# Fourth layer of a graph network: the last 16 node tiles as two groups of 8, and 416 instead of 352 byte pairs on ScalarE in steps 4 to 39

## The reference

```
h = relu(layernorm(x))
layer 0: x += relu((adj @ h) @ W.T + b)
layer 1: x += points and sigmoid attention on a hyperboloid, weighted by adj, normed
layer 2: agg_i = sum_j adj_ij / deg_i * logmap(h_i, h_j)       # Poincare ball, all pairs
         x += expmap(0, agg @ W2 + b2)                          # tanh of the length
layer 3: support = h @ W3;  mask = (adj != 0);  rank = cumsum(mask, axis=1)
         deg = rank[:, -1:];  k = min(deg, 100);  pos = rank - (deg - k)
         w = mask * where(pos > 0, 0.5 ** (k - pos), 0);  x += w @ support + b3
```

## Time and profile before

| | us |
|---|---|
| median of 3 runs | 1047.3 (1044.82 to 1051.48) |
| profiled execution, its own time | 1044.31 |
| its span, first to last instruction | 1042.6 |
| PE busy | 980.6 (94%) |
| DVE busy | 850.0 (82%) |
| ACT busy | 750.8 (72%) |
| POOL busy | 298.0 (29%) |
| mean granted TensorE clock | 0.981 |

### The profile page before, as it was taken

One profiled execution on the slowest core, in us unless ns is written; L12 is line 12 of the kernel. 1 busy time (PEld: TensorE's weight loads), 2 busy tenths in 40 slices (PEclk: granted clock), 3 DMA queues, 4 the chain that ended last, 5 costly groups with the idle time before them and its releaser, 6 DMA issues.

```text
span 1042.6 us, 16458 instructions
## 1 busy us (share of the span) xinstructions
PE 980.6 (94%) x6171; PEld 475.1 (46%) x6171; DVE 850.0 (82%) x1080; ACT 750.8 (72%) x805; POOL 298.0 (29%) x140
## 2 busy tenths in 40 slices
PE   6999979999899999999989999999999999998888
PEld 2444444446644444435434444444455454333455
DVE  6999969998678676697769987878878978888883
ACT  4655545554477667686788989988888888997683
POOL 1069980000001000004015464434343444342001
PEclk9999989999989999999998999999999999999999
DMA  9989987994048899788753444555655553446662
GB/s 330 420 332 422 423 366 241 345 403 162 1 160 282 292 304 301 262 268 303 261 188 127 160 127 158 170 194 164 198 163 162 165 171 116 155 142 201 214 217 78
DMA packets 96350, 238.43 MB, mean 229 GB/s; under 512 B 16401, under 2 KB 45073, under 8 KB 79889
## 3 DMA queue, kind: packets, MB, share of 16 engines
q1 hardware_dynamic: 87056, 220.62, 61.5%
q10 hardware_dynamic: 9216, 16.78, 4.2%
HBM read 219.55 MB, written 17.83 MB: 228 GB/s over the span
## 4 chain that ended last, share of the span: by engine, by line
PE 62%; DVE 20%; ACT 9%; issue 7%; POOL 1%; DMA 1%; DVEq 0%; SPq 0%; ACTq 0%; POOLq 0%
PE PS L577 39%; PE PS L756 9%; DVE TB L1559 6%; PE PS L896 4%; PE PS L865 4%; DVE work L2078 2%; ACT work L1268 2%; ACT work L1276 2%; DVE work L2066 2%; DVE ring L2084 1%; ACT work L1279 1%; DVE work L2072 1%; PE PS L589 1%; DVE work L1729 1%; ACT work L1262 1%
## 5 line engine op out<-in xcount | busy, mean ns | idle before, releaser
L555 POOL TENSOR_TENSOR ring<-work,ring 128x1024 f32<-128x1024 f32 x57 | 135.3, 2374 | 232.8 <-DVE work L2078 232.7
L1729 DVE TENSOR_TENSOR work<-work,ring 128x1024 f32<-128x1024 f32 x128 | 152.9, 1234 | 58.0 <-ACT work L1193 57.9
L1193 ACT ACTIVATE work<-PS,att_sc 128x1024 f32<-128x1024 f32 x128 | 148.0, 1201 | 68.5 <-PE PS L756 59.5
L1118 ACT ACTIVATE work<-PS 128x1024 uint8<-128x1024 f32 x128 | 124.2, 1024 | 100.0 <-PE PS L577 99.9
L577 PE MATMUL PS<-ring,work 128*65 128x256 f32 (+1 forms) x600 | 190.4, 465 | 3.8 <-DVE work L2105 3.8
L577 PE MATMUL PS<-work 128*64 128x512 f32 (+2 forms) x800 | 151.5, 519 | 1.4 <-ACT work L1262 1.2
L2072 DVE SCALAR_TENSOR_TENSOR work<-PS,work 128x1024 f32<-128x1024 f32 x72 | 88.0, 1222 | 55.0 <-PE PS L577 46.5
L756 PE MATMUL PS<-work 128*64 128x512 f16 x1024 | 124.0, 384 | 3.0 <-ACT work L1193 1.6
L577 PEld LDWEIGHTS PS<-ring,work 128*65 128x65 f32 x600 | 80.6, 138 | 90.7 <-issue 65.5
L1268 ACT ACTIVATE work<-work 128x1024 f32<-128x1024 f32 x72 | 76.0, 1055 | 34.8 <-DVE work L2066 34.7
L756 PEld LDWEIGHTS PS<-work 128*64 128x64 f16 x1024 | 59.0, 111 | 79.4 <-issue 34.7
(11 more groups left out here) (280 smaller groups left out, 1402.1 us busy)
## 6 DMA issues: line engine op xcount, KB each, us to landing
ring<-in_adj_t SPq DMA_DIRECT2D x96, 1024.0 KB, 5.4
ring<-in_adj_t SPq DMA_DIRECT2D x104, 512.0 KB, 4.1
work<-in_adj_t SPq DMA_DIRECT2D x32, 1024.0 KB, 8.6
codes<-work ACTq DMA_DIRECT2D x64, 256.0 KB, 7.2
ring<-codes SPq DMA_DIRECT2D x64, 256.0 KB, 4.6
H<-in_adj_t SPq DMA_DIRECT2D x24, 512.0 KB, 4.2
X<-in_x SPq DMA_DIRECT2D x2, 256.0 KB, 5.2
X<-in_x SPq DMA_DIRECT2D x1, 512.0 KB, 10.4
```

Source lines behind the costliest of these rows:

```text
L555: nc.gpsimd.tensor_tensor(near(n), sums(n), near(n), ALU.mult).then_inc(sem("near_ready"), 1)
L1118: nc.scalar.activation(made[:, k, u:HALF:2], PS[:, (4 + 2 * u) * BANK:(6 + 2 * u) * BANK], ACT.Relu).then_inc(sem("codes_made"), 1)
L1193: nc.scalar.activation(att[:, u, :], PS[:, (4 + 2 * u) * BANK:(6 + 2 * u) * BANK], ACT.Sigmoid, bias=att_sc[:, 2:3], scale=att_sc[:, 1:2]) ...
L1729: V.tensor_tensor(prob[:, m % 4, :], att[:, u, :], ring[:, s % RING, u * UNIT:(u + 1) * UNIT], ALU.mult)\
```

## The change

Group (16, 32) becomes (16, 24) and (24, 32). Tiles 16 to 23 are complete after unit 65, so that PE gathers them in unit 69 (nodes2(2)), ACT copies them in unit 70, and DVE does tangent_dot and tangent_scale in unit 71, the other tangent operations behind conversion 1. Every call of steps 3 to 5 above now comes twice, once for 8 tiles each, at new places in the three queues. Group 2 has steps 32 to 47 and group 3 48 to 63, so half 0 is complete only after step 55: the copy on ACT moves behind the conversions, and PE's to_nodes from step 52 to step 60. Apart from that, in steps 4 to 39 ACT converts 416 byte pairs (832 elements) and DVE 608. The last product of groups 1 and 3 uses bank 3, that of group 2 bank 2. Nothing else is changed, and the result is computed as before.

```diff
...
-GROUPS = ((0, 8), (8, 16), (16, 32))
+GROUPS = ((0, 8), (8, 16), (16, 24), (24, 32))
...
 PIECES = ((24, 32), (16, 24), (0, 16))
-COMPLETE = (36, 52, 72)
-COPIES = (2, 4, 7)
+COMPLETE = (36, 52, 66, 72)
+COPIES = (2, 4, 6, 8)
+LAST_BANK = (1, 3, 2, 3)
 VISITS = {38: ("agg2_copied", 2), 41: ("turned_out", 1), 42: ("z_out", 1), 51: ("turned_out", 2), 52: ("z_out", 2),
-  54: ("agg2_copied", 4), 57: ("turned_out", 3), 58: ("z_out", 3)}
+  54: ("agg2_copied", 4), 57: ("turned_out", 3), 58: ("z_out", 3), 69: ("agg2_copied", 6)}
+TANGENTS = (1, 3, 4, 6)
+LASTS = (2, 5, 7, 8)
 CAUGHT = 16
...
 POW_A = 352
+POW_A_EARLY = 416
+
+
+def pairs_a(q):
+    return POW_A_EARLY if 4 <= q < 40 else POW_A
 BF_SHIFT = 7
...
 a, b = GROUPS[q]
-bank = (1, 3 if last else 1, 2)[q]
+bank = LAST_BANK[q] if last else 1
 return PS[:, bank * BANK:bank * BANK + (b - a) * D].rearrange("p (t c) -> p t c", c=D)
...
     a, b = GROUPS[q]
-    bank = (1, 3 if b_row is None else 1, 2)[q]
+    bank = LAST_BANK[q] if b_row is None else 1
     for u in range((b - a) // 2):
...
 def weighted(q):
-    pe.wait_ge(sem("turned_out"), 2 * q + 1)
+    pe.wait_ge(sem("turned_out"), TANGENTS[q])
     through(q, wbd["w2"][:, :], 4)
...
     pe.wait_ge(sem("feats_ready_l3"), q + 1)
-    turn(q, cen, 3 if q == 1 else 0)
+    turn(q, cen, LAST_BANK[q] if q else 0)
 def weighted_last(q):
-    pe.wait_ge(sem("turned_out"), 2 * q + 2)
+    pe.wait_ge(sem("turned_out"), LASTS[q])
     pe.wait_ge(sem("w3_done"), 2)
...
         weighted(1)
+    if n == 69:
+        nodes2(2)
...
+    if q == 1:
+        pe.wait_ge(sem("agg2_copied"), COPIES[2])
+        to_tangent(2)
     if q == 2:
...
     if q == 3:
+        weighted(2)
+    if q == 4:
         pe.wait_ge(sem("far_out"), mirrors(NU - 1))
-        nodes2(2)
-    if q == 4:
         to_last(1)
+    if q == 5:
+        pe.wait_ge(sem("z_out"), TANGENTS[2])
+        nodes2(3)
     if q == 6:
         weighted_last(1)
-    if q == 8:
-        pe.wait_ge(sem("agg2_copied"), COPIES[2])
-        to_tangent(2)
     if q == 10:
-        pe.wait_ge(sem("z_out"), 4)
-        weighted(2)
-    if q == 25:
+        pe.wait_ge(sem("agg2_copied"), COPIES[3])
+        to_tangent(3)
+    if q == 12:
+        weighted(3)
+    if q == 19:
         to_last(2)
-    if q == 27:
+    if q == 21:
         weighted_last(2)
-    if q == 52:
+    if q == 32:
+        pe.wait_ge(sem("z_out"), LASTS[1])
+        to_last(3)
+    if q == 34:
+        weighted_last(3)
+    if q == 60:
         pe.wait_ge(sem("sums_out3_a"), 1)
...
+def last_a(q, k):
+    one("part_a", S3(*GROUPS[q], 0), linear_out(q, True), ACT.Copy, ("through", k))
+
...
         root_part("v_root", "v_norm2", 1, 1)
+    if n == 70:
+        nodes2_out(2)
...
         root_part("ln_sd", "ln_var", 3 * G + 1 + 1, 1)
+    if q == 4:
+        turned_out(2, 4)
+    if q == 5:
+        z_out(2, 4)
+        v_square(2, 4)
     if q == 7:
-        nodes2_out(2)
+        turned_out(1, 5, 3)
     if q == 8:
-        turned_out(1, 4, 3)
-    if q == 10:
-        z_out(1, 4, last=True)
-        part_a(1, 4)
-    if q == 13:
-        turned_out(2, 5)
-    if q == 15:
-        z_out(2, 5)
-        v_square(2, 5)
+        nodes2_out(3)
+        root_part("v_root", "v_norm2", 2, 2)
+    if q == 9:
+        z_out(1, 5, last=True)
+        part_a(1, 5)
+    if q == 12:
+        turned_out(3, 6)
+    if q == 14:
+        z_out(3, 6)
+        v_square(3, 6)
+        ln_square(2)
+    if q == 16:
+        root_part("ln_sd", "ln_var", 3 * G + 1 + 2, 2)
     if q == 19:
-        root_part("v_root", "v_norm2", 2, 2)
-    if q == 26:
-        ln_square(2)
+        root_part("v_root", "v_norm2", 3, 3)
+    if q == 22:
+        turned_out(2, 7, 2)
+    if q == 24:
+        last_a(2, 7)
+    if q == 25:
+        ln_square(3)
     if q == 28:
-        root_part("ln_sd", "ln_var", 3 * G + 1 + 2, 2)
-    if q == 29:
-        turned_out(2, 6)
-    if q == 30:
-        one("part_a", S3(*GROUPS[2], 0), linear_out(2), ACT.Copy, ("through", 6))
-    if q == 56:
-        one("sums_out3_a", TA[:, 0:UNIT], PS[:, 4 * BANK:6 * BANK], ACT.Copy, ("agg3_done", 48),
-            scale=W_SCALE / (F16_TOP / LN_TOP))
+        root_part("ln_sd", "ln_var", 3 * G + 1 + 3, 3)
+    if q == 36:
+        turned_out(3, 8, 3)
+    if q == 38:
+        last_a(3, 8)
...
         act.wait_ge(sem("agg2_near"), NU - 2)
-    both = pw(q).bitcast(I16).rearrange("p (u n) -> p u n", u=2)[:, :, 0:POW_A]
-    nc.scalar.activation(both, code(q).rearrange("p (n u) -> p u n", u=2)[:, :, 0:POW_A], ACT.Copy, scale=BF_STEP)\
+    both = pw(q).bitcast(I16).rearrange("p (u n) -> p u n", u=2)[:, :, 0:pairs_a(q)]
+    nc.scalar.activation(both, code(q).rearrange("p (n u) -> p u n", u=2)[:, :, 0:pairs_a(q)], ACT.Copy, scale=BF_STEP)\
       .then_inc(sem("pw_ready_a"), 1)
...
     power(q)
+one("sums_out3_a", TA[:, 0:UNIT], PS[:, 4 * BANK:6 * BANK], ACT.Copy, ("agg3_done", 56),
+    scale=W_SCALE / (F16_TOP / LN_TOP))
 one("sums_out3_a", TA[:, UNIT:UNIT + BANK], banks(6, 7), ACT.Copy, ("agg3_done", 2 * T),
...
         centre3(1)
+    if n == 71:
+        tangent_dot(2)
+        tangent_scale(2)
...
         dve.wait_ge(sem("agg2_near"), NU - 2)
-    two = code(q).bitcast(U16)[:, POW_A:UNIT]
-    V.tensor_scalar(pw(q)[:, POW_A:UNIT].bitcast(U16), two, 0xFF, BF_SHIFT, ALU.bitwise_and, ALU.logical_shift_left)\
+    a = pairs_a(q)
+    two = code(q).bitcast(U16)[:, a:UNIT]
+    V.tensor_scalar(pw(q)[:, a:UNIT].bitcast(U16), two, 0xFF, BF_SHIFT, ALU.bitwise_and, ALU.logical_shift_left)\
      .then_inc(sem("pw_ready_v"), 1)
-    V.tensor_scalar(pw(q)[:, UNIT + POW_A:2 * UNIT].bitcast(U16), two, 1, 0xFF << BF_SHIFT, ALU.logical_shift_right,
+    V.tensor_scalar(pw(q)[:, UNIT + a:2 * UNIT].bitcast(U16), two, 1, 0xFF << BF_SHIFT, ALU.logical_shift_right,
                     ALU.bitwise_and).then_inc(sem("pw_ready_v"), 1)
...
 power(1)
+tangent_part(2)
+tangent_own(2)
+tangent_sum(2)
+power(2)
 spread3(1)
-power(2)
+power(3)
 feats3(1)
-power(3)
 near2_out(n)
+def last_rest(q):
+    dve.wait_ge(sem("part_a"), q + 1)
+    V.tensor_tensor(S3(*GROUPS[q], 1), linear_out(q, True), S3(*GROUPS[q], 0), ALU.subtract)\
+     .then_inc(sem("parts3_ready"), 1)
+
 def last_passage3(q):
-    if q == 10:
-        tangent_dot(2)
-        tangent_scale(2)
-        tangent_part(2)
-        tangent_own(2)
-        tangent_sum(2)
-        rest3(1)
-    if q == 20:
+    if q == 8:
         length(2)
         tanh_num(2, 0, 5)
-    if q == 21:
+    if q == 10:
         length_root(2)
         tanh_den(2)
+    if q == 11:
         tanh_end(2)
-    if q == 22:
+        rest3(1)
+    if q == 12:
+        tangent_dot(3)
+        tangent_scale(3)
+    if q == 13:
+        tangent_part(3)
+        tangent_own(3)
+        tangent_sum(3)
+    if q == 14:
         step_v(2)
         step_x(2)
-    if q == 23:
+    if q == 15:
         mean3(2)
         centre3(2)
+    if q == 17:
+        spread3(2)
+    if q == 18:
+        length(3)
+        tanh_num(3, 0, 5)
+    if q == 19:
+        feats3(2)
+    if q == 21:
+        length_root(3)
+        tanh_den(3)
+    if q == 22:
+        tanh_end(3)
+    if q == 23:
+        step_v(3)
+        step_x(3)
+    if q == 24:
+        mean3(3)
+        centre3(3)
     if q == 25:
-        spread3(2)
-    if q == 26:
-        feats3(2)
-    if q == 29:
-        dve.wait_ge(sem("part_a"), 3)
-        V.tensor_tensor(S3(*GROUPS[2], 1), linear_out(2), S3(*GROUPS[2], 0), ALU.subtract)\
-         .then_inc(sem("parts3_ready"), 1)
+        last_rest(2)
+    if q == 28:
+        spread3(3)
+    if q == 30:
+        feats3(3)
+    if q == 40:
+        last_rest(3)
```

## The result

The changed kernel takes 1051.88 us (median of 20 runs, 1045.33 to 1057.65), the kernel before, on the same chip, 1047.26 (20 runs, 1044.77 to 1052.21). The ratio is 1.0045 with a 95% interval of 1.0028 to 1.0062, or 4.7 us slower (2.9 to 6.5). That is within 1%, and 1.4 us above the forecast.

The account below looks back on a forecast made before the run. PE was taken to be held in the fourth layer by waits, mostly on DVE, between steps 10 and 29. The sum, +1.4 at step 29 and +1.8 behind it, +3.2 us on the median 1047.3, gave 1050.5 us, range 1044 to 1056.

Parts of the forecast that it names:

- the rival with two low stretches: Fourth layer: the longer PE waits bring one to two more stretches at the low clock, 1052 to 1055 us; chance 0.25.
- Gather in unit 69, +1.8: End of third layer: group 2's gather on PE, ahead of unit 71's scores, lengthens the unit loop by 1.8 us.
- Dot and scale ahead of the entry, +1.8: DVE, unit 71: group 2's two operations ahead of the read-out PE waits for delay its entry by 1.8 us.
- Wait of 2.7 at step 1: Before step 1: PE waits 2.7 us for DVE's tangents of group 2, there at 957.3, turning at 960.0.
- Wait of 4.5 at step 10: Before step 10: PE, ready at 974.8, waits 4.5 us for DVE's tangents of group 3, ready at 979.2.
- the other side: Faster outcome if DVE reaches group 3's tangents early enough at step 10: 1041.3 to 1046 us; chance 0.2.
- Steps 10 to 29, -3.4: Between these steps the change gains: PE's waits fall from 8.1 to 4.7 us, leaving +1.4 at step 29.
- Behind 29, +1.8: After step 29: group 3's turn 0.5, its last product 1.0 and waits 0.3 come now, +1.8 us.
- 416 pairs, nothing: Steps 4 to 39: ACT's extra 3.8 us and DVE's saved 1.3 cancel; same end within 0.1 us as with 352.
- the prediction's three signs of being wrong: PE reaches the second turn after DVE; the unit loop doesn't lengthen; the low clock stands where no wait follows.
- the wait at step 10 is not there: Rival: DVE's 19.2 us to group 3's tangents are 14.8 or fewer, 1046.0 or down to 1041.3 us; chance 0.2.
- The hidden gather: Rival: the gather in unit 69 costs nothing, so 1.8 us fall away, +1.4, 1048.7 us; chance 0.15.

Follow-up runs that it names:

- the reordered change: Changed kernel, groups of 8, gather in unit 69 and 416 pairs kept, with only its fourth-layer calls placed anew; ratio to the kernel before 0.9994.
- the reordered kernel: Kernel before, group of 16 kept, with its fourth-layer calls at other steps on PE, ACT and DVE; ratios to the kernel before 0.9954 and, repeated, 0.9966.

## Why the prediction came out as it did

The side and the size of the time were right: 1050.5 forecast, 1051.9 measured, with most of the chance on a time within 1%. By the stretch, which can be set against the working, the sum has less than half of what was measured: +3.2 forecast, +6.9 in the profiled pair. Of the 3.7 us that it lacks, 1.3 arise ahead of step 10, 2.3 between steps 10 and 29. That the time comes within 1.4 us of the forecast is therefore partly luck; it lies closer still to the 1052 to 1055 of the rival with two low stretches. (The count by waits in the working gives 16.7 - 13.7 = 3.0, not 3.2, which is within its grain.) Point by point:

* **Gather in unit 69, +1.8.** It is 1.73. Right in size. Taking it out was worth 1.4 us of the stretch between the two kernels that differ in nothing else.
* **Dot and scale ahead of the entry, +1.8.** 2.2 us (958.32 to 960.52). The 8-tile product took 1.04 there, not 0.68; it starts while POOL's product of the last unit still runs, for which the working had no term (last section). PE enters 3.9 later (forecast 3.6) and waits 4.66 (4.5).
* **Wait of 2.7 at step 1.** 0.89. DVE was on time: the turn is at +20.7, forecast +20.3. It is PE that came later, with 2.90 and 1.70 us for the gather and step 0 at the low clock. With the entry filled the turn is at +20.7 as well, so this low stretch cost nothing.
* **Wait of 4.5 at step 10.** 4.40, the race that I had named as the point on which the other side depends. The turn is at +40.9, forecast +39.6: DVE's run from step 1 to it is 20.2 us, forecast 19.2, and 0.3 of this is from a longer wait for the root (0.88, not 0.6), another 0.35 from a wait for the near gather (970.28), which the working didn't have. It took the low clock for the turn, and step 10 starts at +41.9, 6.1 later than before (+35.8), forecast 4.8 (979.9 against 975.1 in the addition).
* **Steps 10 to 29, -3.4.** This is the term that was furthest off. Before it is 27.7 us, after 26.6 (988.00 to 1014.6, the second half of the pair that starts at 1013.66): -1.1. Less PE's own 19.1 us, 7.5 are left where I had 4.7. The waits that the timeline shows are 3.1 of them (0.81, 0.22, 0.85, 0.93 and 0.26). The stretch at 1.2 GHz has 2.4: 1.8 on steps 10 and 11 (988.00 to 991.55, where two steps take 1.74 in a row), 0.6 on the weights with their bias row (1.82 us from 991.55, against 1.22 from 971.16). The other 2.0 are too short to be listed one by one; four steps from 1009.50 take 3.91, not 3.5. So the term that was missing is the low clock, which my sum left out and the rival had, and its effect goes on through ACT's queue, where a DVE wait of 3.66 stood that the addition did not have. Filling the wait gave 2.7 us back, moving one square 2.1; both work on the same wait, so they are not added.
* **Behind 29, +1.8.** 1.9 (33.2 to 35.1 us). to_nodes at 60 and DVE's part cost nothing that shows.
* **416 pairs, nothing.** Shown twice, 0.15 and 0.01 us. DVE's gain start to start is 0.016 (0.244 to 0.228), forecast 0.018; ACT's price 0.105, as forecast. The estimate of 17 ns by the Trainium skill, VectorE: DVE Perf Modes, section on the perf-mode tier table, agrees with both.

The rival of two more low stretches took place, both of them, and it had 0.25. Its mechanism was right, its price nearly: nothing for the one at the entry, 2.7 for the one behind step 10, with 1.3 to 2.5 set beforehand for that place. It is also the one of the prediction's three signs of being wrong that came true: the low clock stood where no wait took it up. I held it for the less likely, since before a 2.5 us wait had not brought one; the waits of over 4 us brought one in each kernel that had them (the change, with 352 pairs, with dot and scale moved, with the square moved, with the gather moved, the reordered change at its entry), except where the wait was filled. The rival "the wait at step 10 is not there" fell with 4.40 measured in the trace. The hidden gather fell with 1.73.

What is not settled: the medians differ by 4.7 us (2.9 to 6.5), the stretch by 6.9. The stretch comes from single executions, though it is within 0.25 us in each pair of kernels that differ in nothing or in the split alone (103.55 and 103.70, 96.66 and 96.67, 94.27 and 94.51); the layers ahead scatter by several us from one execution to the next. I can't say whether other executions of the change have a shorter stretch.

## What to carry to other kernels

When work is cut into smaller groups, the question is not how many more instructions there are, but what each call has behind it in its queue: with the same groups, moving calls alone was worth 7.6 us of one stretch (some 5 by time), against 6.9 lost by the change. Then compare like with like: the small groups with their calls well placed belong beside the large groups with theirs well placed, and there they lost 1.4 to 1.7 us. Look for an instruction that waits for another group's result while something ready stands behind it (the square behind L920's copy, the conversions behind part_a), and move the ready one ahead or the waiting one far back. And price a wait on TensorE twice: its own length, and what runs at the low clock behind it, which costs nothing if PE would wait there anyway and more than its own loss if another engine waits for it.

## What the runs showed of the hardware

* A wait of PE of 4.39 to 4.66 us was followed by a low granted clock in every kernel here where it wasn't filled: 0.50 to 0.70 in one of the stretches of 4 us behind it, counted from the sum of unit 69. Waits of 2.5 us at the entry went either way: from 12 to 16 us behind the sum of unit 69 the clock is at 1.00 in the kernel before, in the same with 416 pairs and in the change with dot and scale moved, and at 0.59 in both runs of the reordered one and in the kernel before with its rest at step 36, whose order up to there is that of the kernel before. The Trainium skill, TensorE: Matmul & The Clock Gate, section HAM oscillation, prices a low stretch at its throttled time times one half; the trace agrees for PE's own matmuls (3.62 us for 1.92), but the kernel paid between nothing and 2.7 us for one.
* A low stretch also stood where no long wait explains it: 0.50 behind 12 us of a nearly full PE in the reordered kernel with its entry filled, 0.57 from 12 us behind the sum of unit 69 with the gather moved, after a wait of only 0.80, and 0.89 and 0.69 from +20 in the kernel before, absent in the same kernel with 416 pairs. Of the reordered kernel, unchanged between its two runs, one execution has 0.87 and 0.71 from +20 and the other 1.00, so the place of such a stretch is not the program's alone. What brings these was not found.
* An 8-tile product on DVE (L1942, 128x512, f32) took 1.04 us at 958.32 where 0.68 is usual, and this repeats: 1.03 or 1.04 in each of the five traces that have it in unit 71, 0.68 in the two that have it behind step 1's conversion. POOL's product of the unit runs beside it in the former, from 956.45 to 958.81 here:

```profile
956.45 2.36 POOL L563 TENSOR_TENSOR ring<-work,ring 128x1024 f32<-128x1024 f32 x1 [3.80 <-DVE work L2119]
```

DVE's L2107 (128x1024) shows the same from 860 us on: 0.68 or 0.69 us in the fourteen that start with POOL at rest, 0.86, 1.00 and 1.11 in the three that POOL's product overlaps by 0.32, 0.44 and 0.55 us. So these DVE instructions lose nearly the time that they share with POOL's; no run moves POOL's product alone, so that it is the reason is inferred.
